# Expert blocks on one core: the last loop pass written out, the rows of two blocks put in place on TensorE, and GpSimd's split order changed

## The reference

```
scores = sigmoid(x @ gate.T)                  # 32 experts
the 6 best experts of the 4 best groups of 4; weights normalised, times 2.5
for each expert e:  g = x @ gu[e][:256].T;  u = x @ gu[e][256:].T
                    acc += weight[:, e] * ((silu(g) * u) @ down[e].T)
out = x + acc + shared expert(x)
```

## Time and profile before

| what | us |
|---|---|
| median of three executions (1493.68 to 1499.64) | 1495.8 |
| the profiled execution's own time | 1496.73 |
| its span, first to last instruction | 1494.9 |
| TensorE busy in it | 1426.5 (95%) |
| VectorE busy | 928.4 (62%) |
| ScalarE busy | 631.7 (42%) |
| GpSimd busy | 665.4 (45%) |

### The profile page before, as it was taken

How to read it: one execution, slowest core, us unless ns; L and a number is a source line. 1 busy time by engine, 2 the same in 40 slices (tenths; PEclk the granted TensorE clock), 3 DMA queues, 4 the chain that set the end, 5 groups by cost and what they waited for, 6 DMA issues and landing times. The chain is left out here.

```text
span 1494.9 us, 24234 instructions
## 1 busy us (share of the span) xinstructions
PE 1426.5 (95%) x8980; PEld 1219.1 (82%) x8980; DVE 928.4 (62%) x2102; ACT 631.7 (42%) x1068; POOL 665.4 (45%) x328
## 2 busy tenths in 40 slices
PE   6999999999999999999999999978998999999994
PEld 5999999989899989999998999855775556777772
DVE  6555555545487655578674558767811657888884
ACT  3445345354353444434534435332321125666662
POOL 5006006006274712554930627357600037888874
PEclk9999999999999999999999999989999899999997
DMA  5102003013002012200201300172000679999999
GB/s 209 63 6 88 5 2 127 4 36 121 29 5 90 11 68 82 75 4 23 78 33 50 114 29 1 30 317 84 1 0 11 228 275 292 374 363 368 369 367 324
DMA packets 64402, 177.75 MB, mean 119 GB/s; under 512 B 15155, under 2 KB 32051, under 8 KB 54454
## 3 DMA queue, kind: packets, MB, share of 16 engines
q1 hardware_dynamic: 54134, 152.35, 27.4%
q0 software_dynamic: 10176, 24.12, 6.6%
HBM read 156.78 MB, written 19.66 MB: 118 GB/s over the span
## 5 line engine op out<-in xcount | busy, mean ns | idle before, releaser
L65 PE MATMUL ps_x<-wkv_hi,c_hi 128*128 128x256 f32 (+1 forms) x832 | 241.1, 290 | 0.0
L67 PE MATMUL ps_x<-wkv_hi,c_lo 128*128 128x256 f32 (+1 forms) x832 | 234.2, 281 | 0.0
L66 PE MATMUL ps_x<-wkv_lo,c_hi 128*128 128x256 f32 (+1 forms) x832 | 234.2, 281 | 0.0
L293 POOL TENSOR_TENSOR c_hi<-c_raw,ones 128x1608 fp32r<-128x1608 f32 x30 | 88.3, 2942 | 325.6 <-DMA c_raw<-ctxT 325.6
L773 DVE TENSOR_TENSOR pT<-ps_x,pT 128x512 fp32r<-128x512 f32 (+1 forms) x224 | 145.1, 648 | 124.5 <-ACT pT L617 121.8
L65 PE MATMUL ps_x<-c_hi,wkv_hi 128*128 128x402 f32 x512 | 195.5, 382 | 14.3 <-DVE c_lo L980 12.4
L617 ACT CAST pT<-ps_x 128x512 fp32r<-128x512 f32 (+1 forms) x224 | 124.6, 557 | 168.4 <-PE ps_x L471 165.4
L598 ACT CAST vv<-ps_x 128x512 fp32r<-128x512 f32 (+1 forms) x112 | 62.1, 555 | 278.4 <-PE ps_x L67 278.4
L67 PE MATMUL ps_x<-c_hi,wkv_lo 128*128 128x402 f32 x512 | 177.8, 347 | 0.0
L66 PE MATMUL ps_x<-c_lo,wkv_hi 128*128 128x402 f32 x512 | 177.5, 347 | 0.0
L65 PEld LDWEIGHTS ps_x<-wkv_hi,c_hi 128*128 128x128 f32 (+1 forms) x832 | 153.5, 184 | 17.0 <-issue 17.0
(11 more groups left out here) (321 smaller groups left out, 3058.0 us busy)
## 6 DMA issues: line engine op xcount, KB each, us to landing
e_gu_raw<-w_gu SPq DMA_DIRECT2D x49, 1024.0 KB
c_raw<-ctxT SPq DMA_DIRECT2D x32, 804.0 KB
e_w_dn<-w_dn SPq DMA_DIRECT2D x48, 512.0 KB
x_tok<-slabs SPq DMA_DIRECT2D x13, 1024.0 KB, 4.8
spare<-slabs SPq DMA_DIRECT2D x8, 1024.0 KB, 12.0
h_late<-slabs SPq DMA_DIRECT2D x4, 1024.0 KB, 16.1
e_mix<-shared SPq DMA_DIRECT2D x2, 1536.0 KB, 8.8
wkv_raw<-w_qkv SPq DMA_DIRECT2D x2, 1024.0 KB, 9.0
```

Source lines behind the costliest of these rows:

```text
L65: nc.tensor.matmul(out, a_hi, b_hi, start=start, stop=False)
L66: nc.tensor.matmul(out, a_hi, b_lo, start=False, stop=False)
L67: return nc.tensor.matmul(out, a_lo, b_hi, start=False, stop=stop)
L293: nc.gpsimd.tensor_tensor(c_hi[:, :, chunk(c)], c_raw[:, :, chunk(c)], ones[:, 0:1].unsqueeze(2).to_broadcast([P, KD, CW]), ALU.mult).then ...
```

## The change

The loop takes one turn less. Its last turn is written out behind it on every engine, without what belongs to later blocks: look-ups, gathers, weight loads, token transposes, splits and pick_slots.

The results of the last two blocks (r = 4 and 5) are no longer scattered. VectorE's `put_rows` forms the row that each result goes to, compares it with the 512 token numbers, and writes a one-hot matrix of 128 x 128 for each token tile into pick. TensorE's `put` multiplies each with y in float32 and adds both blocks in four banks of PSUM. SyncE reads acc0 and acc1 once scatters 2 and 3 of the last turn have landed, into buffers that held raw weights; VectorE adds them, then adds the PSUM banks, in place.

GpSimd makes its quarter of the split three blocks ahead instead of two: three are made before the dumps, and a step of its loop is gather(r+6), scatter(r), split_low(r+3) instead of gather(r+6), split_low(r+2), scatter(r). VectorE's three quarters stay two blocks ahead.

```diff
--- before.py
+++ after.py
@@ -1543,6 +1543,7 @@
         w_dn = sb("e_w_dn", [P, U, I // P, D])
         one = sb("e_one", [P, 1])
         rel = sb("e_rel", [P, U, TT])
+        row_at, put_rel = sb("e_row_at", [P, 2]), sb("e_put_rel", [P, 2, TT])
         pick = sb("e_pick", [P, 2, TT, P], F32R)
         facts = sb("e_facts", [P, U, TT, NF], F32R)
         info = sb("e_info", [P, U, NF])
@@ -1556,8 +1557,8 @@
         y = mix[:, 0:U * D].rearrange("p (u d) -> p u d", u=U)
         sg, t1 = (mix[:, U * D + U * I * n:U * D + U * I * (n + 1)].rearrange("p (u d) -> p u d", u=U) for n in range(2))
         hid, hT = (mix2[:, U * I * n:U * I * (n + 1)].rearrange("p (u d) -> p u d", u=U) for n in range(2))
-        part = mix[:, 0:2 * TT * D].rearrange("p (i t d) -> p i t d", i=2, t=TT)
-        out = mix[:, 2 * TT * D:].rearrange("p (t d) -> p t d", t=TT)
+        part = gu_raw[:, 1:3].rearrange("p i k n -> p i (k n)").rearrange("p i (t d) -> p i t d", t=TT)
+        assert TT * D == KD * 2 * I
         raw = mix[:].rearrange("p (s n) -> p s n", s=2)
         mT = mix2[:, 0:KD * T].rearrange("p (k n) -> p k n", k=KD)
         assert 2 * WE == U * (D + 2 * I) == 3 * TT * D and KD * T <= 2 * U * I
@@ -1580,11 +1581,12 @@
         nblk, cblk, base = sb("r_nblk", [P, E]), sb("r_cblk", [P, E]), sb("r_base", [P, E])
         pos = sb("r_pos", [P, TT, E])
         ended, owns, spread = sb("r_ended", [P, E]), sb("r_owns", [P, 1]), sb("r_spread", [P, P])
-        turns_, nturn_f = sb("r_turns", [P, NBLK // U]), sb("r_nturn", [P, 1])
+        turns_, nturn_f = sb("r_turns", [P, NBLK // U - 1]), sb("r_nturn", [P, 1])
         s_sg, s_t1 = (nc.alloc_sbuf_tensor_at(f"r_{n}", [P, 2, T], F32, offset=gu_hi_2 + 8 * T * i) for i, n in enumerate(("sg", "t1")))
         s_hid = sb("r_hid", [P, 2, 2, T])
         ps = ctx.enter_context(nc.psum_tensor("ps_e", [P, 8, 512], F32))
         INFO, XT, GU, HT, DN = range(5)
+        LATE, OUT_BANK = U - 2, (5, 6, 7, INFO)
 
         gu_loaded = [sem(f"e_gu_loaded{i}") for i in range(U)]
         dn_loaded = [sem(f"e_dn_loaded{i}") for i in range(U)]
@@ -1600,6 +1602,7 @@
         zero_done, dump_done, acc_begun, freed = sem("e_zero_done"), sem("e_dump_done"), sem("e_acc_begun"), sem("e_freed")
         part_loaded = [sem(f"e_part_loaded{i}") for i in range(TT)]
         started = sem("e_started")
+        row_at_done, put_rel_done, put_done, put_full, sum_done = (sem(f"e_{n}") for n in ("row_at_done", "put_rel_done", "put_done", "put_full", "sum_done"))
         out_done, stored = sem("e_out_done"), sem("e_stored")
 
         g_loaded, b_loaded, xm_stored = sem("r_g_loaded"), sem("r_b_loaded"), sem("r_xm_stored")
@@ -1621,7 +1624,7 @@
             return raw[:, s, WG:WE].rearrange("p (k n) -> p k n", k=I // P)
 
         def turns(eng):
-            return eng.value_load(nturn_[0:1, 0:1], min_val=T * TOPK // P // U, max_val=-(-MAXB // U))
+            return eng.value_load(nturn_[0:1, 0:1], min_val=T * TOPK // P // U - 1, max_val=-(-MAXB // U) - 1)
 
         def owner(eng, j):
             return eng.value_load(owner_[0:1, bass.ds(j, 1)], min_val=0, max_val=E - 1)
@@ -1687,18 +1690,16 @@
                     down(i, r + U)
                     gate_up(i, r + U + 1)
 
-            wait_turn(sp, added[0], n * (16 * U // 2) + 16)
-            wait_turn(sp, added[1], n * (16 * U // 2))
-            for t in range(TT):
-                sp.dma_start(part[:, 0, t], a["acc0"][P * t:P * t + P]).then_inc(part_loaded[t], 16)
-            wait_turn(sp, added[1], n * (16 * U // 2) + 16)
-            wait_turn(sp, hid_done, n * U + 1)
-            for t in range(TT):
-                sp.wait_ge(part_loaded[t], 16)
-                sp.dma_start(part[:, 1, t], a["acc1"][P * t:P * t + P]).then_inc(part_loaded[t], 16)
+            wait_turn(sp, gu_full, nth(n, 3))
+            for i in range(2):
+                wait_turn(sp, added[i], n * (16 * U // 2) + 16 * (1 + LATE // 2))
+                for t in range(TT):
+                    if i:
+                        sp.wait_ge(part_loaded[t], 16)
+                    sp.dma_start(part[:, i, t], a[f"acc{i}"][P * t:P * t + P]).then_inc(part_loaded[t], 16)
             for t in range(TT):
                 sp.wait_ge(out_done, t + 1)
-                sp.dma_start(a["out"][P * t:P * t + P], out[:, t]).then_inc(stored, 16)
+                sp.dma_start(a["out"][P * t:P * t + P], part[:, 0, t]).then_inc(stored, 16)
             sp.wait_ge(stored, 16 * TT)
 
         @block.gpsimd
@@ -1727,8 +1728,8 @@
             pool.wait_ge(xm_stored, 16)
             for r in range(AHEAD):
                 gather(0, r)
-                if r >= AHEAD - 2:
-                    split_low(0, r + 2 - AHEAD)
+                if r >= AHEAD - 3:
+                    split_low(0, r + 3 - AHEAD)
 
             pool.sem_inc(freed, 3)
             pool.wait_ge(acc_begun, 48)
@@ -1737,11 +1738,16 @@
                 nc.gpsimd.indirect_dma_start(out=a[f"acc{i}"], out_offset=bass.IndirectOffsetOnAxis(ap=dump_row[:], axis=0),
                                              in_=zero[:, 0], in_offset=None, compute_op=ALU.add).then_inc(added[i], 16)
             pool.wait_ge(tables_done, 2)
-            with pool.Fori(0, turns(pool)) as i:
+            n = turns(pool)
+            with pool.Fori(0, n) as i:
                 for r in range(U):
                     gather(i, r + AHEAD)
-                    split_low(i, r + 2)
                     scatter(i, r)
+                    split_low(i, r + 3)
+            for r in range(LATE):
+                scatter(n, r)
+                if r + 3 < U:
+                    split_low(n, r + 3)
 
         @block.vector
         def _(dve):
@@ -1805,6 +1811,16 @@
                 nc.vector.scalar_tensor_tensor(hid[:, b], ps[:, GU, I:2 * I], share[:, b:b + 1], t1[:, b], ALU.mult,
                                                ALU.mult).then_inc(hid_done, 1)
 
+            def put_rows(i, r):
+
+                nc.vector.tensor_tensor(row_at[:, r - LATE:r - LATE + 1], info[:, r, 0:1], far[:, r:r + 1], ALU.add).then_inc(row_at_done, 1)
+                dve.wait_ge(row_at_done, r - LATE + 1)
+                nc.vector.tensor_tensor(put_rel[:, r - LATE], row_at[:, r - LATE:r - LATE + 1].to_broadcast([P, TT]),
+                                        slot[:, P + NBLK:P + NBLK + TT], ALU.subtract).then_inc(put_rel_done, 1)
+                dve.wait_ge(put_rel_done, r - LATE + 1)
+                nc.vector.tensor_tensor(pick[:, r % 2], slot[:, 0:P].unsqueeze(1).to_broadcast([P, TT, P]),
+                                        put_rel[:, r - LATE].unsqueeze(2).to_broadcast([P, TT, P]), ALU.is_equal).then_inc(put_done, 1)
+
             steps = [0]
 
             def link(ins):
@@ -1882,7 +1898,7 @@
             link(nc.vector.tensor_reduce(owns[:], ended[:], AX.X, ALU.add))
             nc.vector.tensor_scalar(spread[:], ident[:], owns[:], float(E - 1), ALU.mult, ALU.min).then_inc(spread_done, 1)
 
-            link(nc.vector.tensor_scalar(turns_[:], slot[:, P:P + NBLK:U], cblk[:, E - 1:E], None, ALU.is_lt))
+            link(nc.vector.tensor_scalar(turns_[:], slot[:, P + U:P + NBLK:U], cblk[:, E - 1:E], None, ALU.is_lt))
             link(nc.vector.tensor_reduce(nturn_f[:], turns_[:], AX.X, ALU.add))
             nc.vector.tensor_copy(nturn_[:], nturn_f[:]).then_inc(tables_done, 1)
             dve.wait_ge(owner_full, 1)
@@ -1907,16 +1923,29 @@
                     turned_low(0, t - 1)
             pick_slots(0, AHEAD)
             hidden(0, 0)
-            with dve.Fori(0, turns(dve)) as i:
+            n = turns(dve)
+            with dve.Fori(0, n) as i:
                 for r in range(U):
                     rows_in(i, r + AHEAD)
                     split_low(i, r + 2)
                     turned_low(i, r + 2)
                     pick_slots(i, r + AHEAD + 1)
                     hidden(i, r + 1)
+            for r in range(U):
+                if r + 2 < U:
+                    split_low(n, r + 2)
+                    turned_low(n, r + 2)
+                if r + 1 < U:
+                    hidden(n, r + 1)
+                if r + 1 >= LATE and r + 1 < U:
+                    put_rows(n, r + 1)
             for t in range(TT):
                 dve.wait_ge(part_loaded[t], 32)
-                nc.vector.tensor_tensor(out[:, t], part[:, 0, t], part[:, 1, t], ALU.add).then_inc(out_done, 1)
+                nc.vector.tensor_tensor(part[:, 0, t], part[:, 0, t], part[:, 1, t], ALU.add).then_inc(sum_done, 1)
+            for t in range(TT):
+                dve.wait_ge(sum_done, t + 1)
+                dve.wait_ge(put_full, t + 1)
+                nc.vector.tensor_tensor(part[:, 0, t], ps[:, OUT_BANK[t]], part[:, 0, t], ALU.add).then_inc(out_done, 1)
 
         @block.scalar
         def _(act):
@@ -1959,16 +1988,28 @@
             turned(0, 1)
             gates(0, 0)
             act.wait_ge(tables_done, 2)
-            with act.Fori(0, turns(act)) as i:
+            def result(i, r):
```

(39 more changed lines are left out.)

## The result

The changed kernel took 1510.79 us (median of 4 runs, 1508.93 to 1510.94) against 1495.14 for the one before (4 runs, 1493.68 to 1499.64): a ratio of 1.0092, 95% interval 1.0079 to 1.0106. It is slower by about 1%, where 1483 was forecast. The profiled execution has a span of 1508.8, 13.9 more than before.

The account below looks back on a forecast made before the run. It took TensorE, busy 95% of the span, as the bound, with VectorE becoming the loop's bound after the change. Sum: 1496.73 - 4.65 + 8.0 - 5.2 - 11.1 = 1483.8, less 0.9: 1483 us; range 1469 to 1520.

Parts of the forecast that it names:

- Step 1: Loop entry: split(2) issued before the dumps ends TensorE's 3.94 wait; third split 0.84 late; gain 4.65 us.
- Step 3: Last pass written out: work for blocks that don't exist goes, 38.7 becomes 33.5; gain 5.2 us.
- The bound of 2: Last pass: 2 us more where GpSimd's split still meets VectorE.
- Step 4: Tail after down(41): products on TensorE replace the last scatters, 11.1 instead of 22.2; gain 11.1 us.
- step 2: Loop: GpSimd's split behind the scatter holds row_out, VectorE becomes the bound at 5.95 per block; +8.0 us.
- rival B: Loop: the split claims the port as the scatter begins; 7.06 per block, +45, total 1520; chance 0.27.

Follow-up runs that it names:

- e4: Changed kernel, order unchanged, with GpSimd's quarter of the split replaced by a zero fill that reads nothing: 1471.24 us, ratio 0.9831.
- e2: Kernel before with only GpSimd's new order (three splits before the dumps, then gather, scatter, split three ahead): 1528.65 us, ratio 1.0217.
- E10: Changed kernel in its own order, with GpSimd splitting one eighth instead of a quarter and VectorE seven eighths: 1490.13 us, ratio 0.9965.
- E3: Changed kernel with the split, still three blocks ahead, placed between gather and scatter: 1493.38 us, ratio 0.9980.
- e6: Changed kernel with order gather, split three ahead, scatter, plus a wait for VectorE's t1_done before each split: 1492.05 us, ratio 0.9967.
- e8: Changed kernel with GpSimd's loop order scatter, gather, split three ahead: 1479.49 us, ratio 0.9889.
- e5: Changed kernel plus a one-column GpSimd zero fill between scatter and split: 1504.36 us, ratio 1.0053.
- e9: Changed kernel with order scatter, gather, split three ahead, and GpSimd splitting one eighth, VectorE seven eighths: 1476.83 us, ratio 0.9860.

## Why the prediction was wrong

Step 1, the entry: the gain is near, 4.06 against 4.65, and the clock dip is gone. But what keeps gate_up(3) late is not what the step said. It had the third split arrive 0.84 late (its own terms, 0.3 + 2.0 + 1.3 behind 1237.12, give 0.6); measured, that split ends at 1242.16, in time, and the 1.49 of waiting come from row_out, held for 2.48. That the sum came near is in part luck. Step 3, the last pass: 3.7 against 5.2. The five intervals up to gate_up(41) took 27.6 instead of 25.8. The last three of them have the held shares: they lie 0.55, 0.57 and 0.97 above those of e4 (5.17, 5.17 and 4.76), where nothing is held. The bound of 2 in that step named it. Step 4, the tail: right, 10.6 against 11.1.

The step that failed is step 2, the loop: forecast 5.95 per block with row_out held, +8.0; measured 6.63, +30.45. The mechanism (the split of GpSimd and VectorE's operations with two SBUF inputs exclude each other) was the right one: e2 puts the whole loss on the order, and e4 removes it with an operation that doesn't read. The hold of row_out that the step forecast for every block happened once, at 1239.71 in front of the loop's steady part. What was wrong is when the exclusion begins. I let the split claim the port at the end of the scatter in front of it. The runs show VectorE locked out while that scatter still runs: e_rel at 1378.58, 0.93 before the scatter's end, and VectorE's own split where it started more than 0.32 behind the scatter. That is rival B (the split claims as the scatter begins), at 1520, which I held at 0.27. The row that decided between the two was in my hands: in the earlier trace rows e_rel starts at 1236.75 and GpSimd's split at 1237.13, and e_rel lost. I set against it the free e_rel at 1464.59 of the earlier trace rows, but there a gather stood behind the scatter, not a split, so that row said nothing against a claim by a split. One row of the very pairing (an indirect DMA's issue, then a split) should have outweighed a row of another.

The Trainium skill, page "SBUF — State Buffer", section "Who interferes with whom", says that whoever issues first holds the shared pair for the whole length of its instruction. By the recorded starts e_rel came first at 1378.58 and lost, so the trace agrees with the rule only if the issue of GpSimd's split lies before its recorded start; the switch of winners at 0.70 to 0.72 before it would put the issue there. E10, where e_pick ends 0.56 before the split in most blocks, doesn't fit a hold for the whole length. Nothing of what the runs above show hangs on these sentences.

Rival B's own price was 7.06 per block, against 6.91 in the 26 held blocks and 5.58 in the seven free ones. I had taken the circle as closed in every block; the trace shows seven blocks in which VectorE's split started before the claim, within 0.32 of the scatter's start, and ran free. On the 33 blocks that is 14 us, and with it B's 1520 becomes about 1506, to which the slower stages named above add some 4.

What I hadn't thought of as a theory is that the hold depends on the phase in which GpSimd settles. E3 and e6 show it: without the direct pair of scatter and split the loop still costs 6.13. In the old order the scatter's wait for the result copy parks GpSimd until VectorE is through with its operations of that kind, and e8 has both: this wait, and the early splits at the entry. That the wait does it is read from these two orders; no run puts such a wait into e3's order and lets it bind.

Still open: what makes the claim. It comes 0.70 to 0.72 before the recorded start of a split behind a scatter that isn't stretched; behind a gather only starts of 0.36 to 0.44 before (lost) and of 0.96 or more before (free) are on record for the quarter split, in e3, e6 and e8. Nor is it settled in e10 which of the two engines gets in when.

## What to carry to other kernels

When an instruction is moved on an engine that is off the critical path, ask less whether it is ready in time than beside what it will now run: here a wait that seemed to cost 0.12 per block was what kept a reading GpSimd operation out of VectorE's busy time, and removing it cost 0.92 per block. Before dropping a wait from a closed circle, look for what it keeps in phase; if the operation behind it has to move, choose its place by when it will start beside the other engine's reads (a gather of 1.0 between scatter and split was worth 31 us in e8, a write of one column only 6 in e5, and a gather in front of a split without the wait left 6.13 in e3), or make it shorter (e10). And of two rows that speak about a mechanism, the one with the same neighbours as the new order decides.

## What the runs showed of the hardware that was not expected

- Behind a scatter, GpSimd's tensor operation is recorded from 0.52 to 0.57 before the end of that indirect DMA's issue (1378.96 against 1379.51); behind a gather, where it waits for nothing, its record opens 0.01 to 0.02 after the end. So a record of 1.86 behind a scatter stands for 1.28 of work.
- A split of VectorE (two SBUF inputs) loses against GpSimd's split when it starts 0.70 or less before the latter's recorded start, and wins from 0.73 on (26 meetings in the changed kernel; 0.32 behind the scatter's start). The smallest operation held, 4 columns, took 2.27 instead of 0.15.
- It works the other way too: beside VectorE's split the gather's issue takes 2.47 instead of 1.00 (e3) and the scatter's 2.19 to 2.37 instead of 1.58 (changed kernel), and a GpSimd split of 0.74 takes 2.52 (e9).
- A write without a read on GpSimd, of the same tile and 0.53 long, holds nobody: 33 splits of VectorE at a mean of 1.753, and e_pick, share and row_out at their usual lengths beside it (e4).
- Two engines that both have room can settle in a stable pattern where they meet in nearly every block: in e3 and e6 five blocks at 6.2 to 6.3, then one at 5.58 or 5.59, over and over.
